# Normalising x on ScalarE in place of VectorE in a four-layer transformer kernel

## What is computed

```
def _layernorm(x, axis=-1, eps=1e-05):
    m = jnp.mean(x, axis=axis, keepdims=True)
    v = jnp.var(x, axis=axis, keepdims=True)
    return (x - m) / jnp.sqrt(v + eps)
...
x = x + _L0_attn_a_ref(_layernorm(x, axis=-1), ...)   # 16 heads of 16, rotary, key mask
x = x + _L0_ffn_ref(_layernorm(x, axis=-1), ...)      # top-1 gated shared k/v attention
x = x + _L0_attn_b_ref(_layernorm(x, axis=-1), ...)   # latent attention, 16 heads
x = x + _L0_ffn_ref(_layernorm(x, axis=-1), ...)      # the same feed-forward layer again
```

## Time and profile before

| | busy us | share of the span | instructions |
|---|---|---|---|
| PE (matmul) | 890.3 | 92% | 6766 |
| PE weight load | 696.7 | 72% | 6766 |
| DVE | 733.7 | 76% | 2379 |
| ACT | 533.5 | 55% | 1410 |
| POOL | 381.6 | 40% | 554 |

### The profile page before, as it was taken

The page is one execution under the profiler, slowest core; times in us unless marked ns, Lnnn a source line. Parts: engine busy times, 40 slices in busy tenths (PEclk is TensorE's granted clock), DMA queues, the critical chain, the costliest instruction groups (busy, mean ns, idle before and its releaser), DMA issues.

```text
span 965.1 us, 20229 instructions
## 1 busy us (share of the span) xinstructions
PE 890.3 (92%) x6766; PEld 696.7 (72%) x6766; DVE 733.7 (76%) x2379; ACT 533.5 (55%) x1410; POOL 381.6 (40%) x554
## 2 busy tenths in 40 slices
PE   5779998989999999978999999999999997999996
PEld 4656776767767776656878888788878776777763
DVE  6668888889889887664766767685867677889973
ACT  6545454543445454526667575757575762554555
POOL 2468788876535443351212112020202000444445
PEclk9789999999999999989999999999999999999999
DMA  6432333331113655001202020202112021132321
GB/s 199 61 54 56 54 45 55 54 55 36 35 35 68 134 109 132 2 16 41 45 1 45 1 44 2 45 2 45 23 23 45 1 34 33 38 62 47 73 48 35
DMA packets 51287, 46.63 MB, mean 48 GB/s; under 512 B 6624, under 2 KB 48624, under 8 KB 51184
## 3 DMA queue, kind: packets, MB, share of 16 engines
q1 hardware_dynamic: 51184, 45.34, 23.4%
HBM read 11.40 MB, written 2.10 MB: 14 GB/s over the span
## 4 chain that ended last, share of the span: by engine, by line
PE 35%; DVE 12%; issue 4%; ACT 1%; DMA 1%; POOL 0%; SPq 0%; POOLq 0%; ACTq 0%; DVEq 0%
PE bank L285 9%; PE bank L1928 5%; PE bank L1878 5%; PE bank L1936 4%; PE bank L1866 3%; DVE weights L1442 3%; DVE q_lo L1422 2%; PE bank L1701 2%; DVE weights L1432 2%; PE bank L1713 2%; DVE arena L1270 1%; PE bank L1698 1%; PE bank L1739 1%; ACT oT L944 1%; DVE rope L1420 1%
## 5 line engine op out<-in xcount | busy, mean ns | idle before, releaser
L1270 DVE TENSOR_REDUCE arena<-bank 128x2 f32<-128x512 f32 (+1 forms) x192 | 128.9, 679 | 27.8 <-PE bank L1701 27.3
L886 ACT ACTIVATE weights<-bank 128x512 f32<-128x512 f32 x144 | 85.7, 596 | 115.4 <-PE bank L1713 114.4
L965 ACT ACTIVATE weights<-weights,neg_max 128x128 f32<-128x128 f32 (+1 forms) x256 | 113.8, 449 | 19.4 <-DVE neg_max L1432 19.4
L1432 DVE CUSTOM_DVE_ANT_0 weights<-bank,arena 128x128 f32<-128x128 f32 (+1 forms) x256 | 80.9, 353 | 56.6 <-PE bank L1928 54.8
L696 POOL TENSOR_SCALAR_AFFINE_SELECT weights<-weights 128x256 f32<-128x256 f32 x144 | 68.3, 475 | 127.4 <-ACT weights L886 127.3
L972 ACT ACTIVATE weights<-bank 128x384 f32<-128x384 f32 x128 | 62.7, 490 | 85.6 <-PE bank L1936 83.4
L1701 PE MATMUL bank<-kf_stack,q_stack 96*128 96x128 f32 (+1 forms) x512 | 109.8, 317 | 0.0
L1928 PE MATMUL bank<-kbT,arena 128*128 128x128 f32 (+1 forms) x512 | 105.1, 328 | 1.1 <-DVE y L420 0.9
L648 POOL TENSOR_SCALAR weights<-weights 128x512 f32<-128x512 f32 x64 | 97.3, 1530 | 13.4 <-ACT weights L789 13.1
L1442 DVE TENSOR_SCALAR weights<-weights,inv_sum 128x128 f32<-128x128 f32 (+1 forms) x256 | 83.8, 370 | 4.5
L285 PE MATMUL bank<-x_hi,wb_hi 128*128 128x256 f32 x256 | 83.4, 326 | 2.8 <-DVE q_lo L1422 2.8
(11 more groups left out here) (232 smaller groups left out, 2412.0 us busy)
## 6 DMA issues: line engine op xcount, KB each, us to landing
q_stack<-q_hi SPq DMA_DIRECT2D x96, 128.0 KB, 3.8
arena<-arena SPq DMA_DIRECT2D x64, 128.0 KB, 2.5
q_stack<-q_lo SPq DMA_DIRECT2D x48, 128.0 KB, 4.0
ka_stack<-k_hi SPq DMA_DIRECT2D x32, 76.5 KB, 3.6
x_all<-x SPq DMA_DIRECT2D x8, 256.0 KB, 5.1
st_wo<-b_wo SPq DMA_DIRECT2D x8, 256.0 KB, 3.9
arena<-b_wqn SPq DMA_DIRECT2D x8, 256.0 KB, 3.4
out<-x_all SPq DMA_DIRECT2D x8, 256.0 KB, 2.1
```

The costliest lines, as they stand in the source:

```text
L886: a.activation(s["pT"][(STEPS * b + k) % N_PT], p2[k % 2][:, :], ACT.Exp).then_inc(s["exp"], 1)
L965: last = a.activation(p, p, ACT.Exp, scale=-1.0, bias=neg_max[:, h % 4, t:t + 1], accum_out=sums[:, h % 4, t:t + 1])
L1270: v.tensor_reduce(into, p1[k % 2][:, :].rearrange("p (h k) -> p h k", h=n), AX.X, ALU.max, negate=True).then_inc(s["maxed"], 1)
L1432: last = v.tensor_tensor_reduce(out=probs[:, h % 4, part], in0=ps_s[h % 2][:, part], in1=mask_b[:, (1 - t) * P:2 * P], scale=1.0, scalar=F ...
```

## The change

`dve_normalize` stays for batches 0 and 1 of the first attention and for the whole second attention. Everywhere else, that is for 6 batches of the first attention and 8 batches of each feed-forward layer, 22 in all, a new function `act_normalize` does the work on ACT: for each half one instruction that adds the negated mean (`Identity` with a bias per partition), then a wait for both, then for each half one that multiplies by `rstd` in place (`Copy` with a scale per partition). POOL negates the mean in a new instruction ahead of the power, for all 32 batches of the four layers. In the first attention ACT does it at step 8, ahead of `high(b + 1, "q")` (DVE did it at step 9); in the feed-forward layers at step 5, ahead of the exponential of that step (DVE did it at step 5). Waits are added so that the shared small tiles aren't overwritten early: `dve_stats` waits for the last `rstd`, `pool_rstd` for the last `xn`.

```
-            per = dict(stats=4, rstd=2, xn=1, xT=1, x_hi=1, x_lo=1, x_done=1, **own)
+            per = dict(stats=4, rstd=3, xn=NT + 1, xT=1, x_hi=1, x_lo=1, x_done=1, **own)
...
+        def last_of(s, name, b):
+            if s is sa or b > 0:
+                return at(s, name, b, 0)
+            of = sa if s is sf[0] else sf[0] if s is sm else sm
+            return at(of, name, B - 1, of["per"][name])
...
         def dve_stats(s, b):
             v = nc.vector
+            v.wait_ge(*last_of(s, "rstd", b))
...
             wait_apart(g, *at(s, "stats", b, 4))
+            g.wait_ge(*last_of(s, "xn", b))
             g.tensor_scalar(var_eps[:, :], mv[:, :, 1], EPS_LN, None, ALU.add).then_inc(s["rstd"], 1)
-            g.wait_ge(*at(s, "rstd", b, 1))
+            g.tensor_scalar(neg_mean[:, :], mv[:, :, 0], -1.0, None, ALU.mult).then_inc(s["rstd"], 1)
+            g.wait_ge(*at(s, "rstd", b, 2))
             g.tensor_tensor(rstd[:, :], var_eps[:, :], expo[:, :], ALU.pow).then_inc(s["rstd"], 1)
+
+        def act_normalize(s, b):
+            act = nc.scalar
+            act.wait_ge(*at(s, "rstd", b, 3))
+            act.wait_ge(*last_of(s, "xT", b))
+            for t in range(NT):
+                act.activation(xn[:, t, :], x_tile(b, t), ACT.Identity, bias=neg_mean[:, t:t + 1]).then_inc(s["xn"], 1)
+            act.wait_ge(*at(s, "xn", b, NT))
+            for t in range(NT):
+                last = act.activation(xn[:, t, :], xn[:, t, :], ACT.Copy, scale=rstd[:, t:t + 1])
+            last.then_inc(s["xn"], 1)
...
         def pe_transpose_x(s, b):
-            nc.tensor.wait_ge(*at(s, "xn", b, 1))
+            nc.tensor.wait_ge(*at(s, "xn", b, NT + 1))
...
# first attention, ACT
+                if k == 8 and b >= 0 and there(b + 2):
+                    act_normalize(sa, b + 2)
                 if k == 8 and there(b + 1):
                     high(b + 1, "q")
...
# feed-forward, ACT
+                    if k == 5 and there(b + 2):
+                        act_normalize(s, b + 2)
...
# first attention, DVE
-                if k == 9 and there(b + 2):
+                if k == 9 and b < 0 and there(b + 2):
                     dve_normalize(sa, b + 2)
...
# feed-forward, DVE
-                    if k == 5 and there(b + 2):
-                        dve_normalize(s, b + 2)
```

More of the change, by code:

```diff
@@ L91, in hybrid_layers_kernel @@
         rstd = sb("rstd", [P, NT])
+        neg_mean = sb("neg_mean", [P, NT])
         xn = sb("xn", [P, NT, D])
@@ L309, in pool_rstd @@
             wait_apart(g, *at(s, "stats", b, 4))
+            g.wait_ge(*last_of(s, "xn", b))
             g.tensor_scalar(var_eps[:, :], mv[:, :, 1], EPS_LN, None, ALU.add).then_inc(s["rstd"], 1)
-            g.wait_ge(*at(s, "rstd", b, 1))
+            g.tensor_scalar(neg_mean[:, :], mv[:, :, 0], -1.0, None, ALU.mult).then_inc(s["rstd"], 1)
+            g.wait_ge(*at(s, "rstd", b, 2))
             g.tensor_tensor(rstd[:, :], var_eps[:, :], expo[:, :], ALU.pow).then_inc(s["rstd"], 1)
+        def act_normalize(s, b):
[8 more added lines that the diff above has]
+            last.then_inc(s["xn"], 1)
         def dve_normalize(s, b):
             v = nc.vector
[L316 to L320, removed]
+            v.wait_ge(*at(s, "rstd", b, 3))
+            v.wait_ge(*last_of(s, "xT", b))
             for t in range(NT):
-                last = v.tensor_scalar(xn[:, t, :], x_tile(b, t), mv[:, t, 0:1], rstd[:, t:t + 1],
-                                       ALU.subtract, ALU.mult)
-            last.then_inc(s["xn"], 1)
+                v.tensor_scalar(xn[:, t, :], x_tile(b, t), mv[:, t, 0:1], rstd[:, t:t + 1],
+                                ALU.subtract, ALU.mult).then_inc(s["xn"], 1 + t)
         def pe_transpose_x(s, b):
-            nc.tensor.wait_ge(*at(s, "xn", b, 1))
+            nc.tensor.wait_ge(*at(s, "xn", b, NT + 1))
             for c in range(NC):
```

## The result

The changed kernel takes 972.41 us (median of 10 runs, 969.79 to 977.14). The kernel before took 964.88 us beside it (median of 10, 963.97 to 966.96). The ratio is 1.008, with a 95% interval of 1.0065 to 1.0095. So the change makes the kernel 7.5 us slower, where 6.5 us faster was forecast. The profiled execution took 972.36 us, with a span of 970.6 us (966.79 and 965.1 before).

The account below looks back on a forecast made before the run. PE, DVE and POOL were near their limits in the first attention; PE set the feed-forward pace. Terms: -9.0 (feed-forward) +1.3 (POOL) +1.2 (head 3) = -6.5, so 965.94 to 959.4 us; own range 955.4 to 963.4, stated range 954 to 969.6.

Parts of the forecast that it names:

- I count the removed DVE work here as 0: First attention: removing DVE's normalising gains 0, since POOL's chain, then ACT's copies, hold PE's transposes anyway.
- 6 x 0.22 = 1.3 us: First attention: POOL's negation lies on the path ahead of the rotation and costs 1.3 us over six batches.
- upper bound of 1.8 us: First attention: most that POOL's negation could cost, at 0.30 us a batch with its semaphore.
- from there it works without a pause up to the quotients `y`: Feed-forward layers, step 5: DVE's 1.07 us of normalising is on the path, worth 0.63 us a batch.
- Seven steady batches: Feed-forward layers, four batches of the second and three of the first: gain 0.63 us each, 4.4 us together.
- together 4.6 us: Seven other feed-forward batches: each gains the smaller of PE's wait and DVE's removed time, 4.6 us in all.
- The other three terms: Gains of 0.85 us in the first feed-forward layer's batch 7, and 0.3 and 0.55 in the second's batches 1 and 3.
- Batch 0 of the first layer: First feed-forward layer, batch 0: falls in the first attention's POOL chain and gains nothing.
- Head 3: Second attention's last batch: ACT's new work behind head 3 pushes PE back by 1.2 us, bounds 0.5 and 1.8.
- The slower one: First attention, step 11: PE's joined idle time brings another half-clock stretch, up to 1.7 us in six batches, 969.6 us; chance 0.14.
- The second rival: Feed-forward layers: the next wait, on DVE's key selection or POOL's mask, takes half the gain, 963.9 us; chance 0.22.
- The table rival: ACT's Identity needs its own table, two more loads a batch, making ACT's block 4.4 us and the kernel 989 us; chance 0.03.

Follow-up runs that it names:

- e1: The kernel before plus POOL's negation of the mean ahead of the power in all 32 batches, its result unread: 968.93 us, ratio 1.0028.
- e8: The changed kernel without POOL's negation, ACT adding the mean itself: 968.55 us, ratio 1.0029 to the kernel before.
- e2: The changed kernel with both feed-forward layers normalised on DVE again, negation kept in all batches: 970.95 us, ratio 1.0052 to the kernel before.
- e7: The kernel before, with DVE normalising one column of each half in the first attention from the third batch on: 966.45 us, ratio 1.0007.
- e4: The kernel before, with DVE normalising only one column of each half in both feed-forward layers: 964.68 us, ratio 0.9994.
- e3: The changed kernel with the first attention as before (DVE normalises, no negation there): 968.16 us, ratio 1.003 to the kernel before.
- e9: The changed kernel with the first attention as before and ACT normalising in the first feed-forward layer only: 968.59 us, ratio 1.003 to the kernel before.

## Why the prediction was wrong

**First attention: the place held, the size did not.** "I count the removed DVE work here as 0" is right (ratio 1.0007 for the one-column kernel), and so is the place: wait on DVE gone, transposes 0.1 us behind ACT, ACT's block hidden (the kernel without the negation is no slower there). The term "6 x 0.22 = 1.3 us" is the one that was mis-sized. By the ratios the negation costs 2.7 us when it is added to the kernel before (e1), and taking it out of the changed kernel brings 4.9 (e8), each with some 2 us either way; the profile shows 4.4 for the whole part. I priced the new instruction by its own duration. The traces show that it takes 0.31 us with its semaphore, and that instructions of POOL fall beside others of DVE. `var_eps` takes 0.50 to 0.60 us in three batches in every profile with the negation ahead of the rotation, with DVE's time freed or not. A rotation takes 2.1 to 2.3 us in place of 1.28 in every one with DVE's time freed (after, e2, e7, e8). My upper bound of 1.8 us had none of that. Over the four batches from mark 3 to mark 7 the stretch from the start of `var_eps` to the rotated q sums to 15.4 us before, 17.0 with the negation alone, 16.5 with DVE's time alone gone (e7) and 17.9 after. So POOL's chain is 2.5 us longer. e2, with the same chain, loses 1.8 us in those batches, and the other 2.2 of the changed kernel's 4.0 go with the stretch at half clock that e2 hasn't.

**Feed-forward layers: the step that failed.** The sentence "from there it works without a pause up to the quotients `y`" was read from a timeline in which DVE indeed has no pause, and from it I concluded that its 1.07 us were on the path. That is the wrong test. The second of DVE's copies at 314.17 needs a result of PE that comes just ahead of it, so the normalising in front of it only filled a wait that is there without it. Seven steady batches were to gain 0.63 us each, 4.4 in all, and lost 0.04 to 0.1 us each. That loss goes with ScalarE's block: in e4 and e1, which don't have it, the same batches change by 0.03 us at most. Where PE waited for DVE's maxima, "together 4.6 us", the gain came in part: 0.6, 0.3 and 0.6 us at marks 9 to 11 and 0.65 at mark 26, in place of 0.5, 1.0, 0.7 and 0.7. The other three terms, 0.85, 0.3 and 0.55, came to 0.2, 0.0 and a loss of 0.1. And the batch that was put at nothing, "Batch 0 of the first layer", lost 1.9 us (e3, e9), by the stretch at half clock. The kernel without the work gives 0.9994, so even what was gained isn't to be found in the time: its profile gains 1.9 us from mark 8 to 15 (148.62 us) and loses 1.5 from 7 to 8 (32.84 us), where the clock falls.

**Head 3: right.** PE waits 1.0 us longer and the batch takes 1.0 us longer (marks 23 to 24), 1.2 forecast.

**The rivals.** The slower one named the right mechanism, one more stretch at half clock when PE's idle time becomes one piece, but put it in six batches at 1.7 us each. It came at the end of the first attention, for 1.9 us, and once inside it, at 101.80 us in the changed kernel's profile, where e2 with the same code hasn't it. The second rival, that the next wait takes up the freed time, is what happened in the feed-forward layers, but in the steady batches it took all, and the next wait was DVE's own for PE's projection, which I hadn't listed. The table rival fell: Identity and Copy alternate 22 times with one load in the trace. The Trainium skill ("ScalarE: Activation LUTs", section "Table sets: the hidden batching unit") puts cheap functions such as copy and identity in every table set, and the trace agrees: one load, 1283 ns.

**The sum as it came out**, by the profiles: +4.4 (first attention) +1.3 (its end) -1.5 (first feed-forward layer) +0.3 (second attention, with 1.0 lost at head 3) -0.2 (second feed-forward layer) +1.3 (start, chance) = +5.6 us, the spans' 5.5. The end is +1.9 for the new stretch at half clock and -0.6 that e1 shows too (30.73 us), in which DVE has all its work; so the -0.6 isn't a gain from the freed DVE. The medians say 7.5; the parts measured alone, 5.4 and 2.6, add to 8.0.

## What to carry to other kernels

That an engine has no idle time ahead of a late result doesn't put its work on the path: check for each instruction behind the removed work when its own inputs come, and leave the work out (one column in place of 256) before moving it, since the move can hardly bring more than that. On the engine whose stream does set the pace, count every small instruction with its semaphore and with what it will meet, and look for a place in the same stream where that engine waits anyway: here moving 1.1 us a batch of POOL's work into such a wait brought 1.1%, while moving 30.5 us of DVE's time cost 0.8%. An engine freed off the path can cost time, by running beside another's work and by letting TensorE run ahead into longer waits. And compare single profiles only where profiles with the same code agree: here marks 3 to 7 (within 0.3 us) and not marks 1 to 7 (within 2.6).

## What the runs showed of the hardware

- VectorE and GpSimd can slow each other, and it isn't always both. An operation of 128 x 2 on POOL took 0.50 us in place of 0.22 beside a `tensor_scalar` of DVE. Two `tensor_tensor`, of 128 x 512 on POOL and 128 x 1056 on DVE, took 2.11 and 2.26 us together in place of 1.28 and 1.24 apart. In e7 DVE's starts 0.06 us ahead of POOL's and takes 1.25 us, and only POOL's takes longer, 2.31. In the earlier trace rows it is the other way round: POOL's rotation keeps its 1.26 us and DVE's two instructions take 2.76 together (elsewhere 0.41 each). In e7 POOL's operation ends 1.1 us behind the end of DVE's, and in the changed kernel DVE's ends 1.1 us behind the rotation ahead of it, as if the later one waited for the earlier. The traces show the times, not the cause.
- Two ACTIVATEs of 128 x 256 with a pointer for bias or scale take 0.91 us together, and the pair that reads the first pair's result starts 0.03 us behind its end.
- The granted clock fell to 0.51 for 3.4 us after PE had been busy 2.44 of 4.5 us (e9), its longest wait 1.31 us, and not after 3.43 of 4.5 (before), with the same work following. One such stretch cost 1.9 us. Its mean over the runs differs between kernels by more than the profiles let one expect (0.970 for the feed-forward part alone, 0.977 with the power moved, 0.973 before), so a comparison of two profiles has to look at it first.
